# One routing piece between steps, a norm spread over a whole unit, and a first stage without its fence

## The reference, cut to what matters

```python
def _L0_ffn_ref(x, ln_w, ff_ln_w, wq, wk, wv, wo, wg, w1, w3, w2):
    h = _rms(x, ln_w)
    q, k, v = h @ wq, h @ wk, h @ wv        # 32 query heads, 8 key heads
    q, k = _rope(q, k)
    attn = softmax(causal(q k^T / 8))
    x = x + (attn v) @ wo
    h = _rms(x, ff_ln_w)
    logits = h @ wg                         # 16 experts
    topv, topi = jax.lax.top_k(logits, 4)
    gate = jax.nn.softmax(topv, -1)
    a = silu(h @ w1[e]) * (h @ w3[e])       # for the chosen experts
    return x + sum(gate * (a @ w2[e]))
...
x = x + 0.5 * _L0_ffn_ref(_layernorm(x), ...)
```

## Time and profile before

| what | value |
|---|---|
| time before | 3854.91 us, median of 3 runs (3842.57 to 3857.17) |
| the profiled execution | 3864.14 us, span 3862.4 us |
| PE busy | 3367.7 us, 87% of the span |
| DVE busy | 2626.8 us, 68% |
| ACT busy | 1929.6 us, 50% |
| POOL busy | 992.1 us, 26% |
| mean granted TensorE clock | 0.91 of 2.4 GHz |

### The profile page before, as it was taken

The page is one execution under the profiler, slowest core; times in us unless marked ns, Lnnn a source line. Parts: engine busy times, 40 slices in busy tenths (PEclk is TensorE's granted clock), DMA queues, the critical chain, the costliest instruction groups (busy, mean ns, idle before and its releaser), DMA issues. The chain is left out here.

```text
span 3862.4 us, 62873 instructions
## 1 busy us (share of the span) xinstructions
PE 3367.7 (87%) x21000; PEld 2229.6 (58%) x21002; DVE 2626.8 (68%) x8701; ACT 1929.6 (50%) x5261; POOL 992.1 (26%) x960
## 2 busy tenths in 40 slices
PE   6899999986995889897899999998699558999975
PEld 4666666664553433343666666665355436878863
DVE  6788888774443776783788888877344466777765
ACT  4567676653221365665566777655222114555531
POOL 3212121333443000011221212133344332122213
PEclk9899999987997688898899999988799669999987
DMA  4231300013754212302060400011655400000010
GB/s 123 91 120 37 129 1 1 34 46 111 157 90 99 68 43 55 69 2 75 15 210 1 163 3 1 4 46 46 180 101 92 126 1 14 1 15 4 1 33 22
DMA packets 203911, 234.63 MB, mean 61 GB/s; under 512 B 20359, under 2 KB 190281, under 8 KB 202825
## 3 DMA queue, kind: packets, MB, share of 16 engines
q1 hardware_dynamic: 172648, 190.48, 16.2%
q0 software_dynamic: 30944, 40.14, 6.2%
HBM read 96.03 MB, written 133.73 MB: 59 GB/s over the span
## 5 line engine op out<-in xcount | busy, mean ns | idle before, releaser
L1723 ACT ACTIVATE p_prob<-bank,p_small 128x256 f32<-128x256 f32 (+3 forms) x1280 | 646.7, 516 | 135.5 <-DVE p_small L1894 128.1
L1894 DVE CUSTOM_DVE_ANT_0 bank<-bank,p_mask 128x256 f32<-128x256 f32 (+3 forms) x1280 | 579.5, 490 | 144.2 <-PE bank L1466 133.5
L2239 POOL TENSOR_TENSOR p_tm<-p_rope_a,p_rope_b 128x512 f32<-128x512 f32 x192 | 246.1, 1282 | 1306.6 <-DVE p_rope_b L1874 1265.8
L1728 ACT ACTIVATE p_prT<-bank 128x512 f32<-128x512 f32 x752 | 426.2, 601 | 256.9 <-PE bank L1475 255.7
L1466 PE MATMUL bank<-p_k,p_q 64*128 64x256 f32 (+3 forms) x3840 | 537.4, 353 | 10.6 <-ACT p_prob L1723 9.4
L1475 PE MATMUL bank<-g_ident,p_prob 128*128 128x128 f32 x3008 | 446.5, 291 | 31.5 <-DVE p_prob L1903 19.0
L1903 DVE TENSOR_SCALAR p_prob<-p_prob,p_small 128x256 f32<-128x256 f32 (+3 forms) x1280 | 418.4, 390 | 11.3
L1484 PE MATMUL bank<-p_prT,p_v 128*64 128x512 f32 (+1 forms) x1504 | 420.0, 602 | 0.3 <-ACT p_prT L1728 0.3
L1475 PEld LDWEIGHTS bank<-g_ident,p_prob 128*128 128x128 f32 x3008 | 343.0, 146 | 121.3 <-issue 45.4
L1466 PEld LDWEIGHTS bank<-p_k,p_q 64*128 64x128 f32 (+1 forms) x3840 | 345.2, 192 | 111.5 <-issue 64.5
L1940 DVE TENSOR_REDUCE p_nmax<-bank 128x1 f32<-128x512 f32 x512 | 325.1, 684 | 100.4 <-PE bank L1525 94.8
(11 more groups left out here) (289 smaller groups left out, 6222.4 us busy)
## 6 DMA issues: line engine op xcount, KB each, us to landing
sorted<-p_blank SPq DMA_DIRECT2D x32, 2304.0 KB, 19.2
p_w<-in_L_ffn_w SPq DMA_DIRECT2D x96, 256.0 KB, 4.5
p_h_in<-sorted SPq DMA_DIRECT2D x158, 144.0 KB, 2.7
p_k_st<-k_saved SPq DMA_DIRECT2D x16, 288.0 KB
p_q_st<-q_saved SPq DMA_DIRECT2D x16, 288.0 KB
g_stage<-in_L_ffn_wq SPq DMA_DIRECT2D x8, 512.0 KB, 4.3
g_stage<-in_L_ffn_wo SPq DMA_DIRECT2D x16, 256.0 KB, 5.2
second_sum<-g_res SPq DMA_DIRECT2D x8, 512.0 KB, 6.0
```

The lines of the kernel that those rows point to most:

```text
L1723: act.activation(s.prob.ap[:, 0:s.o.w], s.use.ap[:, 0:s.o.w], ACT.Exp, bias=sm[:, 0, j:j + 1], scale=-1.0, accum_out=sm[:, 1, j:j + 1]).th ...
L1728: act.activation(s.prT.ap, s.use.ap, ACT.Copy).then_inc(s.use.free[0].sem)
L1894: dve.tensor_tensor_reduce(x, x, A.mask[:, A.mask.shape[1] - o.w:], -1.0, FAR, ALU.add, ALU.min, o.sm.ap[:, 0, h.j:h.j + 1]).then_inc(made)
```

## The change

The diff has four parts. (1) The fence after the first splits is left out in phase 0. (2) `norm_batch` yields once more, between statistics and normed, and is advanced at four places: for batch 1 after pieces 6, 8, 16 and 20 of `prepare(0, 0)`; for batch b + 2 at the start of steps 0, 2, 4 and 6 of unit (0, b) (all four steps of a wide unit). So the two feature steps move there too. (3) In phase 0 SP copies the input from DRAM to DRAM for `res_saved`, and DVE's centring does not wait for it. (4) `beside()` calls `route_on()` once, so routing advances four pieces in a step; in the last unit, which has no pieces beside it, `route_last()` adds four calls, at places between the steps' parts.

```diff
         if roomy:
             yield
-            self.fence()
+            if ph:
+                self.fence()
...
             rooted = self.statistics(norm, [self.res[:, i, :] for i in tiles], LN_EPS, ready)
+            yield
             s = self.step("normed_wide" if wide else "normed", A)
...
-                s.b, s.count = b, self.count(f"p{ph}_saved{b}")
+                s.b, s.count, s.unread = b, self.count(f"p{ph}_saved{b}"), ph == 0
...
         for n_piece, _ in enumerate(prepare(0, 0, made)):
-            if n_piece == 6:
+            if n_piece in (6, 8, 16, 20):
                 next(normed[1])
...
             def beside():
-                route_on()
                 for _ in range(pieces):
                     next(back, None)
                 route_on()
+
+            def route_last():
+                if not nxt:
+                    route_on()
...
-            for t, g in steps:
-                if (t, g) == steps[-1] and c == 0 and b + 2 < B:
+            for n_step, (t, g) in enumerate(steps):
+                if c == 0 and b + 2 < B and n_step * 8 // len(steps) in (0, 2, 4, 6) and n_step % (len(steps) // 4) == 0:
                     next(normed[b + 2])
...
                 if prev:
                     normalise(prev)
+                route_last()
                 beside()
...
+                route_last()
                 beside()
                 if not wide:
                     scores(cur, 2, 3)
+                route_last()
                 for kt in range(0, min(2, nturn)):
                     turn(prev, kt)
...
                 for kt in range(2, nturn):
                     turn(prev, kt)
+                route_last()
                 exponentials()
...
-                w.wait_ge(s.saved, s.ready[t])
+                w.wait_ge(None if s.unread else s.saved, s.ready[t])
...
-            w.wait_ge(*s.ready)
-            sp.dma_start(plan.res_saved[tiles].rearrange("t p d -> p t d"), res[:, tiles, :]).then_inc(s.count.sem, 16)
+            if s.unread:
+                sp.dma_start(plan.res_saved[tiles], x_tiles[tiles]).then_inc(s.count.sem, 16)
+            else:
+                w.wait_ge(*s.ready)
+                sp.dma_start(plan.res_saved[tiles].rearrange("t p d -> p t d"), res[:, tiles, :]).then_inc(s.count.sem, 16)
```

## The result

The changed kernel takes 3807.3 us (median of 4 runs, 3794.81 to 3817.35) against 3856.0 us (median of 4, 3842.57 to 3861.0) for the kernel before on the same chip: a ratio of 0.9877, 95% interval 0.9839 to 0.9916. It is faster by 1.2%, where 3743 us (2.9%) had been forecast, with a range of 3720 to 3800. The profiled execution has a span of 3815.6 us against 3862.4: 46.8 us gained of the 111.6 forecast. By the medians it is 48.7 us.

A forecast was written before the change was run, and what follows sets the result against it. PE was taken to bound the kernel, losing time only when idle or at low clock. Norms 62.1, routing 47.4 and head 2.1 gave 111.6 us off 3864.1: 3752.5 profiled, 3743 median, range 3720 to 3800.

The forecast's parts named there:

- the wide phase: First three units of the wide phase: 117.4 us becomes 102.4 with the norm spread, gain 15.0.
- the routes of step 6: Routes falling on steps 7, 0, 1 of c = 3 units, with over 6 us of DVE room: 0.5 us left.
- (3, 3) longer than before: Last routing unit: takes a route's second half, 1.6 us matmuls, about 2 stall, 1 clock: 4.5 us lost.
- I leave 1.0 us of stall for each unit: Norm units of c = 0: DVE lateness mostly absorbed, 1.0 us stall left; (0, 1) becomes 51.6, gain 8.1.
- 3.0 us of low clock: Unit (0, 0): clock 0.94 over 50.3 us loses 3.0 us, counted within its gain of 6.5.
- I leave 3.0 us of stall and lost clock: Step-2 routes in (3, 1), (3, 2): DVE about 2.6 us late; each unit 56.0 us, gain 10.6.
- rival 3: Slower: a route's square on ACT waits for a row buffer whose sends have not landed; 3%.
- rival 2: Norms gain, routing doesn't: routes wait for each other or POOL, its root behind the key sums; 3791 us, 6%.
- Rival 1: Stalls break up but stay: DVE has under 0.3 us of room in steps 3 and 5; 3799 us, 18%.
- The head, 2.1: Start of the kernel: without the fence POOL's first power starts at 15.65 instead of 17.73, gain 2.1 us.
- The prologue's bound of plus or minus 2: Piece ahead of each phase's first unit: taken as zero, between -2 and +2 us in each of three phases.
- Rival 4: Sends hold up DVE and DVE blocks PE: ten routes give back 80 us, 3823 us; 4%.
- Rival 5: No change to be measured, the slack moves to the experts; 3%.

The follow-up runs named there:

- e4: The changed kernel with the norm's centring part at the start of step 1 instead of step 2 in narrow units: (0, 0) 49.4 us, (0, 1) 54.0 us.
- e7: The changed kernel with norm parts at steps 0, 1, 4, 6, behind the step's scores and normalise: (0, 0) 47.9 us, (0, 1) 51.6 us.
- e11: The changed kernel with late norm parts, four row buffers, split sends, earlier route and one empty turn: 3737.5 us against 3852.5 for the kernel before, 0.9707.
- e5: The changed kernel itself, run on chip C: ratio 0.9855 to the kernel before.
- e9: The changed kernel with a fourth row buffer for the routed tiles: 3807.7 us.
- e10: The changed kernel with a fourth row buffer and the second tile's four sends held back behind the next route's root: 3787.5 us.
- e13: The changed kernel with four row buffers, split sends, a route begun one step earlier and one empty turn: units (3, 1), (3, 2) 57.1 and 57.3 us.
- e1: The kernel before with the spread norm alone: 3864.6 us against 3890.7, ratio 0.9927.
- e12: The kernel before with only the fence in front of the first stage left out: 3856.5 us (single time) against 3852.5.
- e8: The changed kernel with only two of each tile's four sends made: units (3, 1) and (3, 2) 59.5 and 60.1 us.
- e14: The changed kernel with four row buffers, an earlier route and one empty turn, all eight sends together: units (3, 1), (3, 2) 61.7 and 61.5 us.

## Why the prediction was wrong, step by step

**What held.** PE bounds, and only idle PE and a low clock lose time: every unit that lost its stalls came to 49.2 to 49.9 us. (0, 2) 49.2 for 49.3, (3, 0) 49.9 for 49.8, the wide phase 102.0 for 102.4, the routes of step 6, (3, 3) longer than before (59.4 in phase 0, forecast 57.9; in phase 3 57.1 for 56.4 before, where 4.5 more was forecast). POOL's first power at 15.78 for 15.65. No run takes the save alone; in the kernel before no centring instruction of DVE waits 0.2 us or more, so there was no wait to win.

**The step that failed for the norm: "I leave 1.0 us of stall for each unit".** Measured 7.5 us in (0, 1) (58.1 for 49.3 + 1.3) and 8.8 more than the forecast 43.8 in (0, 0). I sized it by DVE lateness absorbed in a roomier step and summed the piece's instructions. What decides is how short the step is and what stands behind the piece in the queue: 2.7 us of DVE work in front of the maxima and the normalise of a step of 4 us. One step earlier it costs 4.1 us less in (0, 1) (e4), and behind the normalise of that step 2.4 less again, which is what I had said (e7, e11: 51.6). In (0, 0) two terms were missing. ACT's copies wait in order for POOL's power (2.54 us, 3.59 in e7). And I had counted 3.0 us of low clock as given back, while the unit's clock is 0.90 in the changed kernel, for 0.94 before, and 0.93 and 0.90 in e7 and e11. I had named DVE's wait for the power before, and not asked who waits for the second one. In phase 0 and phase 3 this is 30.5 us of the 64.8 missing, and e7 brings back 11.9 in phase 0 (against e5 on its chip).

**The step that failed for the routing: "I leave 3.0 us of stall and lost clock" for a route of step 2.** I took it from DVE's room. Measured, unit (3, 1) is 6.6 us over the forecast 56.0 and (3, 2) 7.6, with 7.1 us of stalls from the one step-2 route (1.32, 4.63 and 1.13) in (3, 1), and it is POOL: 10.3 us of sends now reach into the next route's square, mean and root. The rows for it were there. I had worked out the distance for the row buffer (rival 3: some 10 us from one route's sends to the next square) and not for the root, which waits for the whole set and not for the first four. Half of rival 2 was this mechanism (root behind the key sums), at 6% and without the sends. Rival 3's wait did come, at 1.3 us, and hid behind the root (e9). Rival 1 comes nearest in the number (3799 for 3807.3), by another road: its stalls were to come from DVE having no room in steps 3 and 5. e10 and e13 speak against that: with POOL out of the way, and in e13 the route begun a step earlier, the unit comes to 57.1 us for 56.0 (in e10 alone to 59.1). The sum has a slip too: phase 3 was 4.0 us longer before, so the same working gives it a gain of 27.2 and not 24.2, and a forecast of 3740, a little further off.

**The head, 2.1.** Won in full (2.5) and lost again in the prologue's extra work (2.4 in e1); without that work, in the one execution of e12, most of it was lost in unit (0, 0). The prologue's bound of plus or minus 2 was passed by 0.4 in e1; I had taken its middle.

**Rival 4.** The normalise beside sends was as harmless as its row said: in the changed kernel's trace 24 normalise instructions of 512 that overlap a send take 0.50 us in the mean, 228 that overlap nothing of POOL's 0.48. What slows DVE's short operations in the rows above is POOL's arithmetic. Rival 5 found no support.

**The range.** It ended 7 us too low, because its upper end was half the gain by one mechanism, while two small allowances, each for a queue, were short together. With both mechanisms mended the kernel takes 3737.5 us (e11), close to the forecast 3743, but that closeness is luck in good part. Against the kernel before, the norm units of e11 give 18.8 and 17.7 us for the forecast 24.3 and 22.8, the routing units 30.6 and 30.6 for 23.2 and 24.2, and the wide ones 18.4 for 15.0.

## What to carry to other kernels

When a piece is moved into a busy step, price it by the work of that step and by what is queued behind it on each engine on which it has an instruction, not by its own length or by free time elsewhere. The same 2.7 us of DVE made unit (0, 1) 58.1 us long at the head of a short step, 54.0 at the head of the step before and 51.6 behind that step's normalise, and a copy that waits for another engine's power holds up every exponential behind it. When stages of a pipeline are drawn out, work out again for every long job on a shared queue (eight sends, 10.3 us) who is next in that queue, and split the job there: four sends, the root, four sends gave 20 us at no cost that shows. And read a change by units, for the whole time of one trace moves by 10 us and more in stretches that nobody touched. Count the stalls too: the changed routing kept them at some 7 us in the unit that was counted and gained by the clock, with 6.3 us at half rate beside one long gap and three short ones, for 17.3 beside five short ones.

## What the runs showed of the hardware that was not expected

- Two operations of DVE over four numbers per partition last as long as the key sum of POOL that was already running: 0.57 to 0.60 us for 0.16, and 0.65 to 0.66 for 0.17, in units (0, 0) and (0, 1) of both narrow phases. It isn't so for every pair: the centring instructions over 256 numbers beside POOL's power take 0.40 us each.
- Units with whole sends depend on the chip or the time of the run: (3, 1) takes 62.6 us on chips A and D and 67.1 on B and C, and the kernel-before routing of e1 71.7 for 66.6. In e5 a maximum on DVE at 761.80 shows 2.40 us of idle time with no instruction of the core named as its cause, ACT's copy at 766.13 has waited 5.41 us in the same way, and PE then idles 2.52 us at 768.59. The rows, DVE and PE of e5:

```profile
761.80 0.70 DVE L1903 CUSTOM_DVE_ANT_0 bank<-bank,p_mask 128x512 f32<-128x512 f32 x1 [2.40 <-remote]
```
```profile
768.59 1.76 PE L1484 MATMUL bank<-g_ident,p_prob 128*128 128x128 f32 x7 [2.52 <-DVE p_oT_lo L1917]
```

  With half the sends on the same chip (one execution, e8) there is none of it, and on chip D neither the changed kernel nor e14 shows it, so it seems to take both the chip and the sends. What it is stays open; e10 and e13 were not run on such a chip. The old routing has it too (e1), and the ratio of the whole change hardly feels it (0.9877, 0.9855 and 0.9872).
